# A decoder block on one core: feed-forward parts and LayerNorm work given other slots, and one tile copy per odd step given to another engine

## The reference

```
x = x + self_attention(layernorm(x))        # causal, with q, k, v and o weights and biases
x = x + cross_attention(layernorm(x), ctx)  # causal, no weights: q = layernorm(x), k = v = ctx
y = layernorm(x)
logits = y @ W_gate.T ; rw = softmax(top_2(logits))
x = x + relu(y @ W_up.T) @ W_down.T + sum(rw) * (y @ W_expert)
```

## Time and profile before

| | us |
|---|---|
| median of 3 runs | 708.54 (708.42 to 709.91) |
| profiled execution | 706.88 |
| its span in the trace | 705.0 |
| PE busy in the span | 672.6 (95%) |
| DVE busy | 494.4 (70%) |
| ACT busy | 501.6 (71%) |
| POOL busy | 257.1 (36%) |

### The profile page before, as it was taken

How to read it: one execution, slowest core, us unless ns; L and a number is a source line. 1 busy time by engine, 2 the same in 40 slices (tenths; PEclk the granted TensorE clock), 3 DMA queues, 4 the chain that set the end, 5 groups by cost and what they waited for, 6 DMA issues and landing times.

```text
span 705.0 us, 13884 instructions
## 1 busy us (share of the span) xinstructions
PE 672.6 (95%) x4488; PEld 520.1 (74%) x4488; DVE 494.4 (70%) x1730; ACT 501.6 (71%) x1450; POOL 257.1 (36%) x391
## 2 busy tenths in 40 slices
PE   6998999999999999999978988999999999999998
PEld 5776777777877777677756765777767887777786
DVE  6668766766766676767878779978867777764632
ACT  5778877777876778787898878877768876763110
POOL 4745645333555345751654432553202102000100
PEclk9999999999999999999999999999999999999999
DMA  9753533336433464354955776464435344320101
GB/s 315 193 151 75 141 70 91 77 93 184 117 71 91 127 196 98 88 123 124 268 140 144 195 215 144 120 166 104 113 98 156 100 105 106 69 96 1 59 1 60
DMA packets 52326, 86.12 MB, mean 122 GB/s; under 512 B 8608, under 2 KB 16800, under 8 KB 52256
## 3 DMA queue, kind: packets, MB, share of 16 engines
q1 hardware_dynamic: 52256, 85.25, 46.0%
HBM read 27.55 MB, written 7.34 MB: 49 GB/s over the span
## 4 chain that ended last, share of the span: by engine, by line
PE 80%; ACT 7%; DVE 6%; issue 2%; DMA 2%; POOL 2%; SPq 1%; ACTq 0%; POOLq 0%; DVEq 0%
PE t L514 15%; PE m L553 14%; PE m L554 14%; PE m L555 14%; PE pv L547 10%; PE s L500 8%; ACT probs L944 3%; DVE probs L716 2%; PE m L514 2%; ACT prob L953 2%; PE m L619 1%; DMA stack<-stage 1%; POOL probs L1057 1%; PE m L568 1%; DVE prob L726 1%
## 5 line engine op out<-in xcount | busy, mean ns | idle before, releaser
L716 DVE CUSTOM_DVE_ANT_0 probs<-s,mask 128x128 f32<-128x128 f32 (+3 forms) x512 | 246.5, 483 | 124.2 <-PE s L500 122.0
L944 ACT ACTIVATE probs<-probs,negmax 128x128 f32<-128x128 f32 (+3 forms) x512 | 284.7, 559 | 44.3 <-DVE negmax L716 43.6
L514 PE MATMUL t<-ident,probs 128*128 128x128 f32 x1116 | 198.0, 276 | 10.6 <-ACT prob L953 7.1
L500 PE MATMUL s<-stack 96*128 96x128 f32 (+3 forms) x512 | 196.5, 392 | 2.9 <-DMA stack<-stage 1.7
L1057 POOL TENSOR_SCALAR probs<-probs,rsum 128x128 f32<-128x128 f32 (+3 forms) x256 | 133.4, 539 | 176.4 <-DVE rsum L730 176.0
L953 ACT ACTIVATE prob<-t 128x384 f32<-128x384 f32 (+1 forms) x225 | 121.5, 541 | 87.1 <-PE t L514 85.5
L514 PEld LDWEIGHTS t<-ident,probs 128*128 128x128 f32 x1116 | 140.5, 141 | 57.4 <-ACT prob L953 11.0
L500 PEld LDWEIGHTS s<-stack 96*128 96x128 f32 x512 | 97.4, 190 | 14.1 <-DMA stack<-stage 2.4
L944 ACT ACTIVATION_READ_ACCUMULATOR probs<-probs,negmax 128x1 f32 x512 | 99.1, 194 | 0.0
L726 DVE COPY prob<-t 128x256 f32<-128x256 f32 (+1 forms) x215 | 76.3, 355 | 29.8 <-PE t L514 29.1
L553 PE MATMUL m<-xT_hi,w_lo 128*128 128x512 f32 x192 | 78.4, 409 | 1.2 <-DVE xT_lo L784 1.2
(11 more groups left out here) (144 smaller groups left out, 956.6 us busy)
## 6 DMA issues: line engine op xcount, KB each, us to landing
stack<-stage SPq DMA_DIRECT2D x384, 128.0 KB, 2.3
xt<-in_x SPq DMA_DIRECT2D x16, 256.0 KB, 4.2
xres<-in_x SPq DMA_DIRECT2D x4, 1024.0 KB, 6.0
kraw<-in_ctxT SPq DMA_DIRECT2D x16, 256.0 KB, 3.0
cv<-in_ctx SPq DMA_DIRECT2D x16, 256.0 KB, 3.3
x<-xres SPq DMA_DIRECT2D x3, 1024.0 KB, 5.8
res<-x SPq DMA_DIRECT2D x8, 256.0 KB, 6.3
out<-res SPq DMA_DIRECT2D x2, 1024.0 KB, 4.7
```

The source lines that it names most:

```text
L500: nc.tensor.matmul(score_tile(P, i), stack[0:RS, P % 2, h, 0, chunk(qb)], stack[0:RS, P % 2, h, 1, 0:N], start=True, stop=True).then_inc(s ...
L514: mm = nc.tensor.transpose(dst[:, chunk(qb - kb)], probs[:, (2 * P + h) % 3, OFF[qb] + PART * kb:OFF[qb] + PART * kb + PART], ident[:, :])
L716: nc.vector.tensor_tensor_reduce(probs[:, (2 * P + h) % 3, OFF[qb]:OFF[qb + 1]], score_tile(P, i), mask[:, T - N:T], -SCALE, BIG, ALU.add, ...
L944: nc.scalar.activation(tile, tile, ACT.Exp, bias=negmax[:, P % 2, h, qb:qb + 1], scale=-1.0, accum_out=total).then_inc(p_exp, 1)
```

## The change

`act_turns(P)` leaves tile 5 out of ACT's list in the steps of `LIGHT`; the range holds 31, 33, 35, 37 and 39. DVE copies it there, before whatever else DVE has in slot 5. The semaphore counts follow.

```diff
+LIGHT = range(NPS - 1, NPS + PAIRS, 2)
+def act_turns(P):
+    return (0, 1, 4) if P in LIGHT else T_ACT
+def dve_turns(P):
+    return tuple(i for i in range(PAIRS) if i not in act_turns(P))
+ACT_TURNS = [sum(len(act_turns(p)) for p in range(P)) for P in range(NP)]
...
 def turns_at(f):
-    u = feed_start(f)
+    u = feed_start(f) + 1
...
 def gate_at(f):
-    return feed_start(f) + (8 if f == B - 1 else 10)
+    return feed_start(f) + (8 if f == B - 1 else 12)
...
 def up_at(f, m):
-    return gate_at(f) + 4 + (4 if f >= B - 2 else 5) * m
+    return gate_at(f) + 4 + 4 * m + (0 if f >= B - 2 else (m + 1) // 2)
...
 def down_at(f, m):
-    return expert_at(f, KC) + 5 * m if m < 2 else feed_start(f + 1) + 5 * (m - 2)
+    return expert_at(f, KC) + 5 * m if m < 2 else feed_start(f + 1) + 6 * (m - 2)
...
 def stats_slots(j):
-        return [z + 25, z + 28, z + 29, z + 31]
+        return [z + 26, z + 28, z + 29, z + 31]
 def norm_slots(j):
-        return [z + 33, z + 36, z + 36, z + 37]
+        return [z + 35, z + 36, z + 37, z + 38]
 def f_stats_slots(f):
-    return [z + 1, z + 2, z + 4, z + 5]
+    return [z + 4, z + 6, z + 8, z + 8] if f == 0 else [z + 1, z + 2, z + 4, z + 5]
 def f_norm_slots(f):
-    return [z, z, z + 1, z + 1]
+    return [z + 4, z + 5, z + 6, z + 6] if f == 0 else [z, z, z + 1, z + 1]
...
-                    if 0 <= s < NP and i in T_DVE:
+                    if 0 <= s < NP and i in dve_turns(s):
                         turned(s, i)
...
-                    if 0 <= s < NP and i in T_ACT:
+                    if 0 <= s < NP and i in act_turns(s):
                         turned(s, i)
...
+                if s == f_stats_slots(0)[-1] // PAIRS:
+                    f_scale(0)
                 for j in range(B + 1, 2 * B):
```

More of the change, by code:

```diff
@@ L368, in copied @@
         def copied(P, i):
-            if i in T_ACT:
-                return t_act, len(T_ACT) * P + T_ACT.index(i) + 1
-            return t_dve, len(T_DVE) * P + T_DVE.index(i) + 1
+            if i in act_turns(P):
+                return t_act, ACT_TURNS[P] + act_turns(P).index(i) + 1
+            return t_dve, PAIRS * P - ACT_TURNS[P] + dve_turns(P).index(i) + 1
         def emptied(key):
@@ L950, in turned @@
                 act.wait_ge(t_mm, PAIRS * P + i + 1)
-                if P % 2 == 0 and h == 0:
+                if P % 2 == 0 and (h == 0 or i - NT not in act_turns(P)):
                     need(act, pv_done, NT * (P // 2 - 1) + kb + 1)
@@ L1159, in _ @@
                         ln_scale(j)
-                for f in range(B):
+                for f in range(1, B):
                     if s == f_stats_slots(f)[-1] // PAIRS:
```

## The result

The changed kernel takes 713.35 us (median of 8 executions, 712.66 to 715.15), the kernel before 708.48 beside it (8 executions, 706.56 to 711.59): ratio 1.0078, 95% interval [1.0062, 1.0094], 4.9 us slower. The forecast was 710.2 with a range that ended at 712.0: right in direction, and with 1.7 us a third of what came.

The account below looks back on a forecast made before the run. PE, busy 95% of the span, was taken to bound most steps, ACT step 33 and DVE steps 41, 43 and 44. Copies +0.94, joins +0.35 and steps 41 to 47 +0.4 made +1.7 on 708.54: 710.2 us, range 705.5 to 712.0.

Parts of the forecast that it names:

- Steps 31 and 35: DVE's copy of tile 5 delays L811 (step 31) and L838 (step 35), which PE needs: +0.47 us each.
- Step 33: ACT bounds it, but PE waits for tile 4's copy, so moving tile 5's copy gains nothing: 0.
- Steps 37 and 39: L838 late by 0.47 and about 1 us, but other PE work lies ahead of the PV block: 0.
- The landing doesn't move: Start of step 42: step 43's stack tile still lands just before 424.41; PE's wait grows from 0.62 to about 1.4 us.
- The joins, +0.35: Joins of batches 1 and 2: new waits at FL1, FL2 and FG sum to 2.69 and 2.30 us against 2.32 each.
- Steps 44 to 47, +0.2: Step 44 loses 1.42 us of FU parts to 45 and 47; PE reaches step 45's turn 1.2 us earlier: +0.2.
- Part 3: Steps 41 to 47, moved statistics, normalisations and FU parts: +0.4 us with the clock's fall, -0.7 without.
- Statistics, with the fall +0.4: Steps 41 to 44: PV block 0.4 us earlier, DVE's end of step 42 about 0.4 later, one L979 leaving step 43 -0.2.
- B: Rival: the clock doesn't fall in step 42, giving 709.1 us; chance 0.20.
- C: Rival: the copies cost nothing because L811 and L838 have unseen slack, giving 709.3 us; chance 0.13.
- D: Rival: the joins' new waits don't come, giving 705.2 us, halfway 706.9; chance 0.24.
- E: Rival: a second fall of the clock, in step 33 or 51, giving 711.9 us; chance 0.08.

Follow-up runs that it names:

- copy_only: Kernel before with only the copies of tile 5 in steps 31, 33, 35, 37 and 39 moved to DVE: 710.26 us, ratio 1.0019.
- after: The changed kernel with all parts of the change, against the kernel before: 713.35 us, ratio 1.0078.
- copy39: Kernel before with only the copy of tile 5 in step 39 moved to DVE: 709.69 us, ratio 1.0009.
- stats_exp: Kernel before with the statistics' part alone and the expert weight loaded one step later: 708.74 us, ratio 1.0004.
- after_exp: The changed kernel with the expert weight loaded one step later, against the kernel before: 710.01 us, ratio 1.0041.
- joins_only: Kernel before with only the joins' part, new slots in all three feed-forwards: 711.0 us, ratio 1.0030.
- joins_f0: Kernel before with the joins' part for batch 0 alone (FL one slot later, gate and FU two): 708.44 us, ratio 1.0014.
- expert_later: Kernel before with only the 1 MB expert weight loaded one step later in SyncE's queue: 706.95 us, ratio 0.9995.
- stats_only: Kernel before with only the statistics' part (moved statistics and normalisation slots, and f_scale(0)): 710.99 us, ratio 1.0031.
- fl_first: joins_only with VectorE emptying an FL bank at the head of the slot, before its copy; against the kernel before: 709.23 us, ratio 1.0020.
- best: Kernel before with FL0 one slot later in batches 1 and 2, FL banks emptied at slot head, expert weight one step later: 706.98 us, ratio 0.9984.

## Why the prediction was right in sign and too small

The direction was right, and by the terms that were meant to give it. The size was not: three terms of the sum were too small. They are the 0 for step 39 with "the landing doesn't move", the +0.2 for steps 44 to 47, and the +0.2 for the statistics.

- **Steps 31 and 35, +0.47 each**: +0.47 and +0.46. The copy of 384 columns takes 0.56 and 0.47 us until the next instruction, as drawn from the two smaller ones in the earlier trace rows.
- **Step 33, 0**: held; 33 has no new wait in copy_only.
- **Steps 37 and 39, 0 ("a fill part or PE's own work lies ahead of the PV block")**: this failed for step 39. The lateness of `query_lo`, "about 1 us", was right (1.13). But the sentence looked at PE's next use of it and not at SyncE, whose in-order queue waits for it, and the prediction asked about SP only for the moved statistics. In the profiles of after, copy_only and copy39 the tile costs 1.8 to 1.9 us; on average it is less, as far as the times tell.
- **"The landing doesn't move"**: in after it moved by 1.89 us, of which the copy's 1.13 us in SyncE's queue is shown and the rest is not separated from chance. That this tile would be next once the statistics leave step 41 was right, and stats_exp shows what was to be had with the tile early, 1.2 us. That the tile took about half of after's loss is what after_exp shows: without the weight in front of it, 0.41% is left of 0.78%.
- **The joins, +0.35**: +0.17 (steps 51 to the end), each of the three waits as given. For FG in step 52 that is partly luck: the terms that are named there add up to 0.88, and to 1.70 with the two normalisations, not to the 1.26 of the sum; 1.12 + 0.16 came.
- **Steps 44 to 47, +0.2**: +1.4 (joins_only, joins_f0). Part 3 took it that PE would reach the turn at the start of step 45 1.2 us earlier and be held there by no more than the 0.2 that it still owed. PE's step 44 is 1.76 us shorter, VectorE had 0.26 us to spare, and PE waited 0.71 us (0.9 in time) at that turn. The wait in step 47, 0.18 us, was not foreseen at all. These waits came alike in every kernel that has the joins' part for batch 0.
- **Statistics, with the fall +0.4**: that sum held the joins' +0.2, so the statistics stood at about +0.2. With the tile early stats_exp has -1.20 in steps 40 and 41 and +1.96 in 43 and 44, which is +0.8, and with step 42 taken against expert_later +1.1. The step that failed is "DVE's end of step 42 moves by about +0.4": in stats_exp PE waits 2.12 us for a normalised tile at the head of step 43. In after the statistics' share of steps 43 and 44 is +1.6 (-0.06 against joins_only's -1.71).
- **The clock**: it fell again in after, as the forecast had it at two to one, and stayed low for 6.8 us instead of 3.4 (0.72 in step 42). Rivals B, C and D did not come. E put a second fall in step 33 or 51, where none came; its 711.9 was the nearest figure, by another cause.

In the profiled execution the failing terms together are 1.9 us at the tile, 1.2 in steps 44 to 47 and about 1.4 of the statistics. Added to the forecast of 1.7 they give 6.2, against 6.7 of that profile from step 30 on. But it is the slowest of eight, and the median lost 4.9, so the terms are not to be taken as averages. Open: how the 0.31% of stats_only split, since its profiled execution had slow transfers; how the tile's half of after's loss divides between the copy's delay and late transfers; and whether step 39 alone costs anything by the times, its interval holding 1.

## What to carry to other kernels

An instruction that is set back on one engine delays each queue that waits for it. Ask of SyncE's queue as well as of the next matmul, above all where large loads stand behind it on full DMA engines. Where PE's work is taken out of a step in which another engine is nearly full, PE comes to its next wait for that engine sooner and gives the time back there; where the work arrives it costs its full length. Where two waits end together, the profile names one, and removing that one alone can show nothing.

## What the runs showed of the hardware

The same program, in the same place, met different landing times. joins_f0 does nothing new ahead of step 42, yet its tile for step 43 landed 17.1 us after step 40's start and PE waited 3.24 us; joins_only, the same up to there, waited 0.62.

```profile
429.01 0.48 PE L500 MATMUL s<-stack 96*128 96x128 f32 x1 [3.24 <-DMA stack<-stage]
```

The kernel before ranged from 705.4 to 713.5 us over all groups, with mean granted clocks from 1.000 at the fast end to 0.990 at the slow one. A wait like this, with the lower clock behind it, may be one source of that spread; only profiled executions show it. So a step of one profile that hangs on a transfer among full DMA engines is not a price until a second execution has it; steps that hang on engines alone repeated to 0.05 us (45 to 47 of joins_only, joins_f0, fl_first, after and after_exp: +3.11 to +3.15).

On the clock, windows of step 42: 0.82 in before and 1.00 in expert_later, each behind waits of about 0.85 and 0.62 us, and 0.72 in after, behind 3.56. The length of the wait doesn't order them: copy_only has 0.81 behind 2.54 us, and best, the second line, 0.73 behind 0.85 and 0.10.

```profile
424.72:432.96 8.24, 6.90 (x65) 4.57 (x65) 8.06 (x29) 6.26 (x21) 3.18 (x4) 1.00 0.85 247
...
426.83:437.00 10.17, 9.15 (x65) 5.67 (x65) 8.07 (x29) 6.27 (x21) 3.17 (x4) 0.73 0.85 217
```

The Trainium skill ("TensorE: Matmul & The Clock Gate", part 1) has the clock fall when the engine has been idle, and a watch that runs free of the kernel. The traces fit the second: the same short waits had a fall in one execution and none in the other. They don't bear out the first by itself, since best's clock fell with no wait above 0.90 us in the 7 us ahead of it.
